# The weighting of the low one-hots in the edge-counting stage: from GpSimd to VectorE

## What is computed

```python
edge_index = jnp.stack([src, dst])
x = x + _L0_gnn_ref(_layernorm(x), edge_index, edge_weight, ...)      # attention over edges
x = x + _L0_ffn_ref(...)                                              # mixture of experts
x = x + _L1_gnn_ref(_layernorm(x), edge_weight, ...)                  # agg[dst] += x[src] * edge_weight
x = x + _L1_ffn_ref(...)
x = x + _L2_gnn_ref(...)                                              # three attention layers over edges
x = x + _L2_ffn_ref(...)
x = x + _L3_gnn_ref(...)                                              # twice agg[dst] += edge_weight * h[src]
x = x + _L3_ffn_ref(...)
```

## Time and profile before

| | |
|---|---|
| median of three runs | 5162.18 us (5162.09 to 5163.13) |
| the profiled execution | 5158.9 us, of which the span from first to last instruction is 5157.2 us |
| busy over the span | PE 81%, PEld 70%, DVE 47%, ACT 36%, POOL 19% |
| mean granted TensorE clock | 0.891 of full |
| counting stage, first one-hot to last copy from PSUM | 753.2 to 1089.3 us, 6.5% of the span |
| instructions of the stage that the change touches | 125 each of L878, L896 and L897 |

### The profile page before, as it was taken

How to read it: one execution, slowest core, us unless ns; L and a number is a source line. 1 busy time by engine, 2 the same in 40 slices (tenths; PEclk the granted TensorE clock), 3 DMA queues, 4 the chain that set the end, 5 groups by cost and what they waited for, 6 DMA issues and landing times. The chain is left out here.

```text
span 5157.2 us, 79633 instructions
## 1 busy us (share of the span) xinstructions
PE 4193.0 (81%) x22693; PEld 3607.3 (70%) x22694; DVE 2448.4 (47%) x4164; ACT 1862.9 (36%) x3203; POOL 974.6 (19%) x921
## 2 busy tenths in 40 slices
PE   2799889964659985958997997997599869899675
PEld 2677768853548754857886886885499758788554
DVE  5555569964330022136985995996411140210424
ACT  2443325542310132425665664665143310110322
POOL 2666646623500001210000000000122200000101
PEclk8788889977979987989998998998699989999788
DMA  3554424432343112322221221221222243133000
GB/s 105 125 120 117 116 60 173 185 119 63 106 144 149 62 34 66 104 67 49 59 44 41 56 59 27 58 57 37 76 70 68 67 134 151 65 151 149 13 18 27
DMA packets 469286, 437.46 MB, mean 85 GB/s; under 512 B 357428, under 2 KB 421641, under 8 KB 456350
## 3 DMA queue, kind: packets, MB, share of 16 engines
q1 hardware_dynamic: 433918, 338.42, 21.8%
q0 software_dynamic: 35232, 97.61, 6.7%
HBM read 341.00 MB, written 94.92 MB: 85 GB/s over the span
## 5 line engine op out<-in xcount | busy, mean ns | idle before, releaser
L2599 PE MATMUL p_acc<-p_H,p_eT 125*125 125x256 f32 x3750 | 823.6, 378 | 0.0
L2599 PEld LDWEIGHTS p_acc<-p_H,p_eT 125*125 125x125 f32 x3750 | 695.3, 187 | 106.0
L1395 PE MATMUL p_acc<-p_message,p_spread 125*125 125x260 f32 x1666 | 429.0, 425 | 30.1 <-issue 30.1
L2083 DVE BATCH_NORM_STATS2 features_stats<-F x60 | 29.2, 486 | 871.7 <-ACT F L2074 868.9
L1142 POOL DMA_INDIRECT p_message<-edge_table,p_index x425 | 403.7, 950 | 192.3 <-issue 121.7
L1395 PEld LDWEIGHTS p_acc<-p_message,p_spread 125*125 125x125 f32 x1666 | 350.6, 212 | 100.7 <-issue 32.0
L1854 ACT ACTIVATE p_hid<-p_up,p_b1s 128x125 f32<-128x125 f32 x764 | 273.0, 366 | 396.6 <-PE p_up L1830 353.3
L1830 PEld LDWEIGHTS p_up<-p_xT,p_w1s 128*128 128x128 f32 x3056 | 376.7, 199 | 51.4 <-issue 32.4
L1830 PE MATMUL p_up<-p_xT,p_w1s 128*128 128x125 f32 x3056 | 384.5, 283 | 32.8 <-issue 13.3
L1838 PE MATMUL p_down<-p_w2s,p_hid 128*125 128x256 f32 x1528 | 358.9, 384 | 7.6 <-ACT p_hid L1854 6.4
L526 PE MATMUL p_turned<-identity,p_slot 125*128 125x125 f32 x400 | 88.5, 373 | 293.3 <-DVE p_slot L494 289.3
(11 more groups left out here) (495 smaller groups left out, 7026.0 us busy)
## 6 DMA issues: line engine op xcount, KB each, us to landing
sums_first<-edge_sums SPq DMA_DIRECT2D x39, 1562.5 KB
p_count<-edge_counts SPq DMA_DIRECT2D x375, 152.6 KB
p_second<-edge_sums SPq DMA_DIRECT2D x36, 1562.5 KB, 8.1
edge_sums<-p_sums SPq DMA_DIRECT2D x25, 1562.5 KB
edge_counts<-p_total SPq DMA_DIRECT2D x25, 683.6 KB
p_w1s<-in_L_ffn_W SPq DMA_DIRECT2D x16, 1024.0 KB
p_got<-made SPq DMA_DIRECT2D x25, 560.0 KB
p_dst_all<-dst_row SPq DMA_DIRECT2D x25, 531.2 KB, 4.2
```

Of the source, the lines that this page charges most:

```text
L1395: last = pe.matmul(at, spread[:, k], message[0:P, m, k], start=(k == 0), stop=(k == R_CH - 1))
L2599: last = pe.matmul(acc[:, s, 0:C], eT[:, r % 4, a % 4], H[:, a, 0:C], start=(a == 0), stop=(a == T - 1))
```

## The change

The GpSimd program of the stage is dropped. VectorE does the same multiplication, by the same helper and over the same 128 x 625 numbers, right behind the two comparisons of the batch. The wait for `low_ready` comes along with it, now on the engine that makes `low`; the semaphore `heavy_ready` that TensorE waits for is now raised by VectorE. Nothing else differs: tile sizes, buffers, the order of TensorE, ScalarE and SyncE.

```diff
@@ -878,10 +878,6 @@
             eng.tensor_tensor(heavy[:, at, :, 0:P], low[:, at], own.edges[:, bass.ds(n * KB, KB), 2:3].bitcast(F32).to_broadcast([EB, KB, P]),
                               ALU.mult).then_inc(heavy_ready, 1)
 
-        @block.gpsimd
-        def _(pool):
-            over_batches(pool, lambda n, k, i: weighs(pool, n, k))
-
 
         @block.vector
         def _(dve):
@@ -895,6 +891,7 @@
                 dve.wait_ge(batch_summed, n + 1)
                 dve.tensor_tensor(low[:, at], lanes(P), each(own.low, n, P), ALU.is_equal).then_inc(low_ready, 1)
                 dve.tensor_tensor(cell[:, at], lanes(P), each(own.key, n, P), ALU.is_equal).then_inc(cell_ready, 1)
+                weighs(dve, n, k)
 
             def one_and_tile(n, k, i):
                 one(n, k, i)
```

## The result

The changed kernel takes 5120.83 us (median of four runs, 5117.51 to 5124.76) against 5162.14 us before (median of four, 5154.70 to 5163.13): the ratio is 0.9923, with a 95% interval of 0.9906 to 0.9941. In two later comparisons, each with runs of the kernel before around it, it was 0.9931 (0.9915 to 0.9948) and 0.9932 (0.9918 to 0.9945). In microseconds the three differences of medians are 41.3, 37.1 and 35.5; the forecast was 39.2.

What follows compares the result with a forecast made beforehand. The counting stage was taken as bound by VectorE and GpSimd taking turns. Per group 5.19 us of holds go and 3.60 us of multiplications come; 39.2 us in all, 5162.2 - 39.2 = 5123.0 us, range 5115 to 5136.

Steps and rivals of the forecast that it cites:

- The hold is GpSimd's: Counting stage: VectorE's two-input `low` stands still until GpSimd's multiplication ends, 1.84 us against 0.80, 100 of 125 times.
- Holds removed: Per group on VectorE: four held batches lose 1.04 us each, L904 to L907 1.03 us, together 5.19 us.
- Multiplications added: Five weightings a group on VectorE, 0.72 us each from start to start, 3.60 us a group.
- upper bound of 0.95: Weighting on VectorE if its added wait for `low` shows in full: 0.23 us on top of 0.72.
- lower one of 0.65: Least cost of a weighting on VectorE: what a held `low` needs behind GpSimd's end, 0.66 us.
- cover of 0.64 us: What remains of `cell` after `low` ends, hiding the weighting's wait; called three times the 0.15 us latency.
- A group of 11.71 us: VectorE's group after the change: 15 x 0.72 + 0.57 + 0.34 us, against 13.31 before.
- turn of the loop: VectorE between groups at the loop's end: adds 0.18 us in both kernels.
- TensorE next: TensorE needs 11.05 us a group against VectorE's 11.71; at the last batch it lags 0.2 us more.
- Sum: Whole stage: 24 x 1.59 + 4.16 - 2.88 = 39.4 us, less 0.2 us lag, gain 39.2 us.
- C: Rival: TensorE becomes the bound at a lower clock, some 4.3 us a batch, 190 us more, 5313; chance 0.01.
- D: Rival: nothing comes of it, since a store or ScalarE stands right behind; no change, chance 0.02.

## Why the prediction was right, point by point

- *The hold is GpSimd's.* Shown: it goes with GpSimd's multiplication, comes back with another GpSimd instruction that reads (at the two-input VectorE instruction that comes up while it runs), and stays away with one that writes.
- *Holds removed, 5.19 us a group; L904 down to 0.42, to its follower 0.57.* Both as written: 0.42 and 0.57. The prediction takes GpSimd's 1.62 us as its own work, of which part looks like standing still behind `cell`. The sum doesn't hang on it, since the whole 1.62 us go.
- *Multiplications added, 0.72 us each, wait hidden.* 0.72 in the trace, 0.71 by doubling. The upper bound of 0.95 is what another order of the lines costs (0.96 measured); the lower one of 0.65 was met nowhere. The cover of 0.64 us is four times the 0.15 us of the latency, and not three times as the prediction has it.
- *A group of 11.71 us.* The first is 11.71 (767.05 less 755.34). But the mean of the first 24 is 11.84 (1039.62 less 755.34, over 24), where the prediction's turn of the loop would make it 11.80. The mis-sized term is the loop's turn: the prediction had 0.18 us for both kernels, read from one turn of the kernel before. A group without a turn behind it takes 13.31 us before and 11.71 after. The eleven with one take 13.48 (0.17 more), and after 12.06 the first time and 12.00 the other ten (0.35 and 0.28 more). Together that is 1.3 us more than before. The hold of L904 has nothing to do with it: without weighting, where L904's counterpart takes 0.42 us, the turn costs 0.17 as before. All traces with the weighting in VectorE's loop show 0.28 to 0.29, except those in which the wait for `shared` is long fulfilled. What in the longer loop costs the 0.11 us was not tried.
- *TensorE next, 0.2 us more lag at the end.* 0.26 and 0.19 us, by its start and by the last store. Its pace of 2.21 us a batch is what the stage without weighting and the one with ScalarE's help run at.
- *Sum.* 38.1 us in the stage against 39.2: the 1.1 us that are missing are the turns of the loop, 1.3, less 0.1 to 0.2 for writing 1.60 us a group as 1.59.
- *Stages behind move as a block.* Their instructions are the same; the time from the last store to the end of the span was 4067.8 us before and 4069.7, 4061.1 and 4061.0 in the three traces of the changed kernel. The differences between traces of one program are larger than that between the two kernels, so nothing can be said below some 8 us there.
- Rivals C and D: the clock stayed at 0.99, and neither a store nor ScalarE bounds the stage even at 281 us. The price of C was added up wrongly: 125 batches of 4.3 us are 537 us against the 297 predicted, 240 more and not 190. Its chance of 0.01 doesn't depend on that.

## What to carry to other kernels

A busy engine may be standing still. When one line has two durations for the same shape, look which other engine's instruction ends a fixed time before each long one: moving that work onto the "busier" engine can free more time than it adds, here 5.19 us a group for 3.60. Work added to the engine that bounds the stage costs its distance from start to start (0.71 us here, where 0.80 is recorded). A wait on an instruction of the same engine cost nothing with one other of 0.72 us between, and 0.24 us with none. Before moving work off the bound, measure the next one by leaving the work out: here 17 us were left, and moving one small operation a group to ScalarE took them all.

## What was not expected of the hardware

- The hold seems to go both ways: GpSimd's multiplication ends 1.09 to 1.10 us behind the end of the `cell` that it started beside (625 columns), or 0.67 to 0.68 (375 columns), whether it started 0.27 us into that instruction or 0.16. Its recorded 1.62 us are then not its own cost. What it takes with nothing of VectorE beside it was not measured; an addition of the same 128x625 numbers on GpSimd, elsewhere in the kernel before (L2189), took 1289 to 1518 ns.
- The turn of a hardware loop costs VectorE 0.17 us before and without weighting, 0.28 (0.35 the first time) in the changed kernel, and nothing that shows where the instruction that waits at the loop's end finds its semaphore long raised.
